# Attention kernel on eight cores: at each head change the next head's key and value expansion is placed behind the current step's work on the tensor engine

## The chip, the cores and the metric

The kernel runs on all 8 cores of one Trainium2 chip. There is no communication between the cores: each works on its own 1024 query rows. The metric is device time in microseconds (us) of the slowest core, lower is better. A core has five engines with a queue each, which run side by side and meet through semaphores: TensorE (PE, with its weight loads listed apart as PEld), VectorE (DVE), ScalarE (ACT), GpSimd (POOL) and SyncE (SP).

## The reference

One layer on x of shape (2, 4096, 4096): latent attention with 32 heads, then a gated low-rank feed-forward, each followed by a residual add and a layer norm. The part around the change:

```python
q = _rmsnorm(x @ wq_a.T) @ wq_b.T                 # 32 heads of 128
ckv, k_pe = split(x @ wkv_a.T)                    # latent of 256, rope part of 64
kv = _rmsnorm(ckv) @ wkv_b.T                      # per head: 64 of k_nope, 128 of v
q_pe, k_pe = rope(q_pe), rope(k_pe)
k_full = concat([k_nope, broadcast(k_pe)])        # 128 per head
scores = einsum('bqhd,bkhd->bhqk', q_full, k_full) * softmax_scale
attn = softmax(where(causal, scores, min))
out = einsum('bhqk,bkhd->bqhd', attn, v)
x = layernorm(x + out @ wo.T)
x = layernorm(x + ffn(x))                         # router, top 16 of 64 experts, rank 8
```

## The kernel before

The kernel runs in stages divided by barriers of all engines: the latent of keys and values (A), the queries (B and C), attention (D), the output projection with the first layer norm, and the feed-forward. The change is in stage D alone. `K` and `V` are not stored for all heads; only the normalised latent `cnorm` (256 x 4096) is, and each head's keys and values are expanded from it shortly before they are used. `emit_expansion(h, bank)` does that in 8 blocks of 512 keys. A block has 2 matmuls for the 64 k_nope rows into the left half of a PSUM score bank, a copy of them on DVE into `Kf`, 8 matmuls for four 128-key pieces of V into the right half of the bank, and a copy of them on ACT into `Vx`. In each block PE waits for the copies of the block ahead, since both use the same bank. `Kf` and `Vx` have two buffers, by the parity of the head.

Attention itself is one flat list of steps, `iters`: 32 heads, 8 slots of 128 queries, and 1, 2, 3, 4, 1, 2, 3, 4 key blocks of 1024 for them, so 20 steps a head and 640 in all. Step r has four parts: QK(r), 2 matmuls of 512 columns into `scores[r % 2]` (`sA` or `sB`); exp(r), one ACT instruction of 128x1024 into `P_sb`; T(r), 8 transposes on PE into `ptP`; evac(r), a copy of them (with a mask in a slot's last step) into `PT_sb`, on DVE if r is even or the step is the last of its slot, otherwise on ACT; and PV(r), 8 matmuls of 128x129 that add up in `mix`. Behind a slot's last PV there is a finish: reciprocal and scaling on DVE, a transpose on PE, and a copy back into `Q` on DVE.

The order within each queue is the order in which the Python loop emits. Round r of the loop emits exp(r) on ACT, then QK(r+1), PV(r-1) and T(r) on PE, then the finish of r-1 if there is one, then evac(r). So QK runs one step ahead of the exp, and PV one step behind the transposes. Where steps r and r+1 belong to different heads (r = 19, 39, ...; 31 times), `emit_expansion` of the next head goes between exp(r) and QK(r+1). Its score bank is the one that QK(r+1) will write, so PE waits for exp(r-1) ahead of it. In this text the steps around such a head change are called by the numbers of the first one: step 18 is r-1 (neither first nor last in its slot, its evac is on DVE), step 19 is the head's last (evac with mask, on DVE), and steps 20 and 21 are the next head's first two.

Every instruction is recorded by one helper, so the profile gives line 267 for all; the tiles tell them apart. `sA`, `sB` in the output of a matmul is QK or the expansion, `mix` is PV (or, with `idn`, the finish), `ptP` is a transpose; `AR` is the SBUF arena that holds all the rest.

Of the kernel before, what the change touches and what calls it, by code (L numbers as in the profile page):

```python
# [294 lines left out]
def build(debug=False, race_detect=True, upto="F"):  # L295
# [56 lines left out]
    with ExitStack() as ctx:  # L352
        em = Em(nc, ctx)
        _LAST_EM[0] = em
        _emit(nc, em, d, ctx, debug, upto)
        _replay(nc, em, ctx)
# [3 lines left out]
def _emit(nc, em, d, ctx, debug, upto="F"):  # L360
# [332 lines left out]
    with ExitStack() as pctx:  # L693
# [9 lines left out]
        scores = [sA, sB]  # L703
# [27 lines left out]
        tok_exp = [None] * N  # L731
# [8 lines left out]
        def emit_expansion(h, bank):  # L740
            hp = h % 2
            war = tok_flash_done.get(h - 2)
            ev = []
            kn_ev = [None] * 8
            v_ev = [None] * 8
            em.waits("pe", [t_wkvb])
            for b in range(8):
                if b >= 1:
                    em.wait("pe", kn_ev[b - 1])
                for c in range(2):  # L750
                    em.opw("pe", [t_wkvb], "matmul", bank[0:64, 0:512],
                           wkvb_sb[c][:, h * 192: h * 192 + 64],
                           cnorm[c][:, b * 512:(b + 1) * 512],
                           start=(c == 0), stop=(c == 1))
                t_kn = em.mark("pe")
                em.waits("dve", [t_kn, war, t_init, t_init_p])
                em.op("dve", "tensor_copy", Kf[hp][0:64, b * 512:(b + 1) * 512],
                      bank[0:64, 0:512])
                kn_ev[b] = em.mark("dve")
                ev.append(kn_ev[b])  # L760
                if b >= 1:
                    em.wait("pe", v_ev[b - 1])
                for sub in range(4):
                    kk = b * 4 + sub
                    for c in range(2):
                        em.opw("pe", [t_wkvb], "matmul",
                               bank[:, 512 + sub * 128: 512 + sub * 128 + 128],
                               cnorm[c][:, kk * 128:(kk + 1) * 128],
                               wkvb_sb[c][:, h * 192 + 64: h * 192 + 192],
                               start=(c == 0), stop=(c == 1))  # L770
                t_v = em.mark("pe")
                em.waits("act", [t_v, war, t_init, t_init_p])
                dst = Vx[hp][:, b * 4 * VSTRIDE:(b + 1) * 4 * VSTRIDE]
                dst = dst.rearrange("p (s w) -> p s w", w=VSTRIDE)[:, :, 0:128]
                em.op("act", "copy", dst,
                      bank[:, 512:1024].rearrange("p (s w) -> p s w", w=128))
                v_ev[b] = em.mark("act")
                ev.append(v_ev[b])
            tok_exp_ready[h] = ev

        def emit_qk(it):
            cu = iters[it]
            par = it % 2
            hp = cu["h"] % 2
            if it - 2 >= 0:
                em.wait("pe", tok_exp[it - 2])
            em.waits("pe", tok_exp_ready.get(cu["h"], []))
            kb = cu["kb"]
            lhsQ = Q[:, cu["h"] * 1024 + cu["s"] * 128: cu["h"] * 1024 + cu["s"] * 128 + 128]
            for hh in range(2):  # L790
                em.op("pe", "matmul", scores[par][:, hh * 512:(hh + 1) * 512],
                      lhsQ, Kf[hp][:, kb * 1024 + hh * 512: kb * 1024 + hh * 512 + 512],
                      start=True, stop=True)
            tok_qk[it] = em.mark("pe")
# [4 lines left out]
        for r in range(N + 1):  # L799
            prev = iters[r - 1] if r >= 1 else None  # L800
            cur = iters[r] if r < N else None
            nxt = iters[r + 1] if r + 1 < N else None

            if cur is not None:
                par = r % 2
                em.wait("act", tok_qk[r])
                if r - 2 >= 0:
                    em.wait("act", tok_pvt[r - 2])
                em.op("act", "activation", P_sb[par][:], scores[par][:], AF.Exp,
                      scale=SCALE)  # L810
                tok_exp[r] = em.mark("act")

            if nxt is not None:
                if cur is not None and nxt["h"] != cur["h"]:
                    if r - 1 >= 0:
                        em.wait("pe", tok_exp[r - 1])
                    emit_expansion(nxt["h"], scores[(r + 1) % 2])
                emit_qk(r + 1)

            if prev is not None:  # L820
                parp = (r - 1) % 2
                sp = prev["s"] % 2
                em.wait("pe", tok_evac[r - 1])
                if prev["first"] and fin_done[sp] is not None:
                    em.wait("pe", fin_done[sp])
                em.waits("pe", [fin_act_prev[0]])
                hpp = prev["h"] % 2
                kbp = prev["kb"]
                for t in range(8):
                    em.opw("pe", [tok_evac[r - 1]], "matmul", pv_[sp],  # L830
                           PT_sb[parp][:, t * 128:(t + 1) * 128],
                           Vx[hpp][:, (kbp * 8 + t) * VSTRIDE:
                                     (kbp * 8 + t) * VSTRIDE + 129],
                           start=(prev["first"] and t == 0),
                           stop=(prev["last"] and t == 7))

            if cur is not None:
                em.wait("pe", tok_exp[r])
                if r - 2 >= 0:
                    em.wait("pe", tok_evac[r - 2])  # L840
                for t in range(8):
                    em.opw("pe", [tok_exp[r]], "transpose",
                           ptP[par][:, t * 128:(t + 1) * 128],
                           P_sb[par][:, t * 128:(t + 1) * 128], idn16[:])
            tok_pvt[r] = em.mark("pe")

            if prev is not None and prev["last"]:
                sp = prev["s"] % 2
                h_, sf = prev["h"], prev["s"]
                em.wait("dve", tok_pvt[r])  # L850
                if fin_pe_prev[0] is not None:
                    em.wait("dve", fin_pe_prev[0])
                em.op("dve", "reciprocal", rcp_c, pv_[sp][:, 128:129])
                em.self_edge("dve")
                em.op("dve", "tensor_tensor", att_tm, pv_[sp][:, 0:128],
                      rcp_c.broadcast_to((128, 128)), op=ALU.mult)
                t_fin = em.mark("dve")
                fin_done[sp] = t_fin
                em.waits("pe", [t_fin, fin_act_prev[0]])
                em.opw("pe", [t_fin], "transpose", atp, att_tm, idn16[:])  # L860
                t_atp = em.mark("pe")
                fin_pe_prev[0] = t_atp
                em.wait("dve", t_atp)
                em.op("dve", "tensor_copy",
                      Q[:, h_ * 1024 + sf * 128: h_ * 1024 + sf * 128 + 128],
                      atp)
                fin_act_prev[0] = em.mark("dve")
                if sf == NSLOT - 1:
                    tok_flash_done[h_] = fin_act_prev[0]

            if cur is not None:
                e = "dve" if (cur["last"] or r % 2 == 0) else "act"
                em.wait(e, tok_pvt[r])
                if cur["last"]:
                    fam = 0 if cur["s"] < 4 else 1
                    em.op(e, "tensor_tensor", PT_sb[par][:], ptP[par][:],
                          mask2[:, fam * 1024:(fam + 1) * 1024], op=ALU.mult)
                elif e == "act":
                    em.op(e, "copy", PT_sb[par][:], ptP[par][:])
                else:  # L880
                    em.op(e, "tensor_copy", PT_sb[par][:], ptP[par][:])
                tok_evac[r] = em.mark(e)

        em.barrier()
        if debug:
# [408 lines left out]
```

How the kernel before makes its waits and increments, by code:

```python
        def body(h):  # L264
            for entry in em.stream[e]:
                meth, args, kw, sem, n = entry[:5]
                ins = getattr(h, meth)(*args, **kw)
                for s, v in (entry[5] if len(entry) > 5 else ()):
                    ins._wait_ge(s, v)
                if sem is not None:
                    ins.then_inc(sem, n)
```

## Time and profile before

| | us |
|---|---|
| median of 2 timed runs | 4754.3 (4746.57 to 4762.03) |
| profiled execution, device time | 4605.99 |
| its span, slowest core (core 2) | 4604.3 |
| spans of the 8 cores | 4536.6 to 4604.3 |
| stage D on core 2, from the first expansion to the last finish | 1155 to 3400 |

The profile comes from one execution. Busy times are sums over instructions of an engine, and they overlap between engines. In the timeline a row is a group of like instructions in order of start: start in us from the start of the span, time it took, engine, operation, output and input, and count; in square brackets is the engine's idle time ahead of it, and what ended that.
### The profile page before, as it was taken

The page shows a single profiled execution, that of the slowest core. Times are in us where ns is not written, and L with a number is a line of the kernel's source. Part 1 is how long each engine was busy: PE and PEld are TensorE (multiplying, and loading weights), DVE is VectorE, ACT ScalarE, POOL GpSimd, SP SyncE. Part 2 cuts the span into 40 slices and gives each one's busy share as a digit, 9 for nine tenths or more (in the row PEclk, how much of TensorE's full clock was granted, in tenths as well). Part 3 has the DMA queues.
Part 4 walks back from the last instruction along what each step waited for, and adds up shares of the span by engine and source line. Part 5 has one row for each costly group of instructions (what it writes and reads, how often), then busy time and mean ns, then how long its engine had stood idle before and what let it go on. Part 6 is the DMA issues. An engine that isn't in the chain of part 4 may idle for free.

```text
span 4604.3 us, 53278 instructions; the slowest of 8 cores (4536.6 to 4604.3 us)
## 1 busy us (share of the span) xinstructions
PE 2833.6 (62%) x19214; PEld 1381.0 (30%) x19214; DVE 1019.7 (22%) x1923; ACT 1229.8 (27%) x1280; POOL 355.1 (8%) x466
## 2 busy tenths in 40 slices
PE   2772644444666676666666666666668888727650
PEld 0220211111333343333333333333333333302110
DVE  0110010000232323222322322223310000161117
ACT  0000001111444444444454444444420000000110
POOL 4431002233000000000000000000010000000000
PEclk9886877777899989999999999899999999957775
DMA  8877240001100000000000000000043333210003
GB/s 119 114 100 107 40 67 6 0 0 25 22 1 1 1 1 1 1 1 1 1 1 1 1 1 1 1 1 1 1 75 82 83 83 82 55 38 0 0 0 146
DMA packets 76490, 145.64 MB, mean 32 GB/s; under 512 B 12306, under 2 KB 53396, under 8 KB 70228
## 3 DMA queue, kind: packets, MB, share of 16 engines
q0 software_dynamic: 67792, 116.29, 15.6%
q1 hardware_dynamic: 8452, 25.95, 1.5%
q8 instruction: 169, 2.77, 0.2%
q14 instruction: 77, 0.63, 0.0%
HBM read 233.31 MB, written 16.78 MB: 54 GB/s over the span
## 4 chain that ended last, share of the span: by engine, by line
PEldq 32%; issue 18%; PEld 15%; DVE 15%; ACT 7%; DMA 4%; another core or an unknown queue 3%; DVEq 2%; POOL 2%; POOLq 2%; ACTq 1%; SPq 0%
PEldq L267 32%; DVE AR L267 15%; ACT AR L267 7%; PEld mix L267 4%; PEld psE L267 3%; PEld sA L267 3%; DVEq L267 2%; POOL AR L267 2%; POOLq L267 2%; PEld psL L267 1%; ACTq L267 1%; DMA AR<-wqbT 1%; DMA AR<-xoT 1%; DMA out<-AR 1%
## 5 line engine op out<-in xcount | busy, mean ns | idle before, releaser
L267 PE MATMUL sA<-AR 128*128 128x128 bf16 (+2 forms) x3200 | 527.4, 288 | 194.1 <-issue 58.0
L267 PE MATMUL mix<-AR 128*128 128x129 bf16 x5120 | 410.1, 223 | 260.8 <-DVEq L267 172.9
L267 PE MATMUL psE<-AR 128*128 128x512 bf16 x2048 | 479.1, 398 | 16.8 <-issue 10.5
L267 PEld LDWEIGHTS mix<-AR 128*128 128x128 bf16 x5120 | 312.1, 99 | 572.1 <-DVEq L267 375.2
L267 PE MATMUL ptP<-idn,AR 128*128 128x128 bf16 x5120 | 401.8, 223 | 37.6 <-ACTq L267 37.3
L267 ACT ACTIVATE AR<-sB,consts 128x1024 bf16<-128x1024 f32 x320 | 356.3, 1113 | 147.4 <-PEq L267 118.9
L267 ACT ACTIVATE AR<-sA,consts 128x1024 bf16<-128x1024 f32 x320 | 356.2, 1113 | 91.2 <-PEq L267 71.0
L267 ACT COPY AR<-ptP 128x1024 bf16<-128x1024 bf16 x192 | 194.3, 1012 | 638.6 <-PEq L267 638.6
L267 ACT ACTIVATE AR<-AR 128x1024 bf16<-128x1024 bf16 (+3 forms) x76 | 76.4, 1006 | 1043.5 <-DVEq L267 1043.5
L267 PEld LDWEIGHTS ptP<-idn,AR 128*128 128x128 bf16 x5120 | 322.6, 99 | 48.3 <-ACTq L267 48.1
L267 PEld LDWEIGHTS sA<-AR 128*128 128x128 bf16 (+1 forms) x3200 | 199.2, 101 | 413.0 <-issue 389.1
L267 PEld LDWEIGHTS psE<-AR 128*128 128x128 bf16 x2048 | 206.0, 102 | 290.1 <-issue 74.1
L267 DVE TENSOR_TENSOR AR<-ptP,AR 128x1024 bf16<-128x1024 bf16 x256 | 177.1, 692 | 375.6 <-PEq L267 367.5
L267 PE MATMUL psL<-AR 128*128 128x512 bf16 (+1 forms) x768 | 186.9, 409 | 90.3 <-DMA AR<-xT 83.5
L267 ACT CAST AR<-sA 128x512 bf16<-128x512 f32 x256 | 149.8, 585 | 334.7 <-PEq L267 334.7
L267 DVE CAST AR<-sA 64x512 bf16<-64x512 f32 x256 | 174.8, 683 | 266.2 <-PEq L267 260.4
L267 DVE COPY AR<-ptP 128x1024 bf16<-128x1024 bf16 x192 | 132.8, 692 | 418.6 <-PEq L267 410.8
L267 PE MATMUL sB<-AR 128*128 128x512 bf16 x640 | 201.2, 397 | 26.0 <-issue 0.2
L267 PE MATMUL psC<-AR 128*128 128x512 bf16 x512 | 174.2, 516 | 66.9 <-DMA AR<-wqbT 60.0
L267 PE MATMUL mix<-idn,AR 128*128 128x128 bf16 x256 | 55.8, 218 | 246.7 <-DVEq L267 246.7
L267 POOL DMA_DIRECT2D AR<-A_sta x32 | 16.9, 664 | 2244.5 <-DVEq L267 2244.5
L267 PE MATMUL psB<-AR 128*128 128x512 bf16 x512 | 114.3, 385 | 107.0 <-DMA AR<-wqaT 107.0
(91 smaller groups left out, 1733.1 us busy)
## 6 DMA issues: line engine op xcount, KB each, us to landing
AR<-xT POOLq DMA_DIRECT2D x256, 128.0 KB, 11.4
AR<-wo_sta POOLq DMA_DIRECT2D x32, 1024.0 KB, 8.6
AR<-xoT SPq DMA_DIRECT2D x32, 512.0 KB, 8.3
AR<-xoT POOLq DMA_DIRECT2D x32, 256.0 KB, 21.7
AR<-wqaT POOLq DMA_DIRECT2D x4, 2048.0 KB, 69.1
AR<-wqbT POOLq DMA_DIRECT2D x8, 1024.0 KB, 29.8
out<-AR SPq DMA_DIRECT2D x16, 512.0 KB, 2.6
out<-AR POOLq DMA_DIRECT2D x16, 512.0 KB, 2.9
```

Of the source, the lines that this page charges most:

```text
L267: ins = getattr(h, meth)(*args, **kw)
```

## The change

At a head change the expansion of the next head and QK(r+1) move from ahead of PV(r-1) and T(r) to the end of the round, behind PV(r-1), T(r) and the emission of evac(r). Nothing is added or removed, and all other rounds are as they were. On PE the order at a head change goes from expansion, QK(20), PV(18), T(19), QK(21) to PV(18), T(19), expansion, QK(20), QK(21). On DVE evac(19) goes from behind the 8 key copies to ahead of them. The order on ACT stays.

```diff
-            if nxt is not None:
-                if cur is not None and nxt["h"] != cur["h"]:
-                    if r - 1 >= 0:
-                        em.wait("pe", tok_exp[r - 1])
-                    emit_expansion(nxt["h"], scores[(r + 1) % 2])
+            boundary = (nxt is not None and cur is not None
+                        and nxt["h"] != cur["h"])
+            if nxt is not None and not boundary:
                 emit_qk(r + 1)
 
             if prev is not None:
@@
                     em.op(e, "tensor_copy", PT_sb[par][:], ptP[par][:])
                 tok_evac[r] = em.mark(e)
+
+            if boundary:
+                if r - 1 >= 0:
+                    em.wait("pe", tok_exp[r - 1])
+                emit_expansion(nxt["h"], scores[(r + 1) % 2])
+                emit_qk(r + 1)
```

## Rows read from the trace of the kernel before

**Rows 1.** The page: its first line, and the busy times of all engines.

```profile
span 4604.3 us, 53278 instructions; the slowest of 8 cores (4536.6 to 4604.3 us)
PE 2833.6 (62%) x19214; PEld 1381.0 (30%) x19214; DVE 1019.7 (22%) x1923; ACT 1229.8 (27%) x1280; POOL 355.1 (8%) x466
```

**Rows 2.** Busy time by stretch, core 2: from second to last expansion, with column heads.

```profile
core 2: us, PE busy (x) PEld busy (x) DVE busy (x) ACT busy (x) POOL busy (x), PEclk, DMA share, GB/s
1230.27:3325.89 2095.62, 1400.84 (x13440) 814.26 (x13441) 618.85 (x1380) 990.52 (x1021) 0.00 (x0) 0.97 0.00 1
```

**Rows 3.** Waits of PE in the same stretch: total us, times, longest us.

```profile
PE mix L267 <- DVEq L267: 392.2, 618, 1.3
PE ptP L267 <- ACTq L267: 34.7, 58, 0.9
```

**Rows 4.** Timeline of core 2 into one head change, PE, ACT and DVE.

```profile
1998.93 0.60 PE L267 MATMUL sB<-AR 128*128 128x512 bf16 x2
1998.96 1.01 ACT L267 COPY AR<-ptP 128x1024 bf16<-128x1024 bf16 x1 [3.83 <-PEq L267]
2000.07 1.11 ACT L267 ACTIVATE AR<-sA,consts 128x1024 bf16<-128x1024 f32 x1
...
2000.13 0.62 PE L267 MATMUL mix<-AR 128*128 128x129 bf16 x8 [0.61 <-ACTq L267]
...
2001.34 1.11 ACT L267 ACTIVATE AR<-sB,consts 128x1024 bf16<-128x1024 f32 x1 [0.16 <-issue]
2001.35 0.61 PE L267 MATMUL ptP<-idn,AR 128*128 128x128 bf16 x8 [0.59 <-ACTq L267]
...
2002.04 1.31 PE L267 MATMUL sA<-AR 128*64 128x512 bf16 x10
2002.08 0.69 DVE L267 COPY AR<-ptP 128x1024 bf16<-128x1024 bf16 x1 [4.48 <-PEq L267]
...
2002.96 0.68 DVE L267 CAST AR<-sA 64x512 bf16<-64x512 f32 x1 [0.19 <-issue]
2003.52 0.59 ACT L267 CAST AR<-sA 128x512 bf16<-128x512 f32 x1 [1.07 <-PEq L267]
```

**Rows 5.** Timeline of core 2 behind that expansion.

```profile
2016.23 0.59 PE L267 MATMUL sA<-AR 128*128 128x512 bf16 x2 [0.87 <-ACTq L267]
...
2016.90 0.63 PE L267 MATMUL mix<-AR 128*128 128x129 bf16 x8
2016.94 1.11 ACT L267 ACTIVATE AR<-sA,consts 128x1024 bf16<-128x1024 f32 x1 [0.88 <-PEq L267]
...
2017.37 0.61 PE L267 MATMUL ptP<-idn,AR 128*128 128x128 bf16 x8
...
2018.06 0.60 PE L267 MATMUL sB<-AR 128*128 128x512 bf16 x2
2018.11 0.69 DVE L267 TENSOR_TENSOR AR<-ptP,AR 128x1024 bf16<-128x1024 bf16 x1 [2.77 <-PEq L267]
...
2018.98 0.62 PE L267 MATMUL mix<-AR 128*128 128x129 bf16 x8 [0.31 <-DVEq L267]
...
2019.44 0.61 PE L267 MATMUL ptP<-idn,AR 128*128 128x128 bf16 x8
```

**Rows 6.** Busy time by stretch, core 2: three heads, from expansion to next expansion.

```profile
1230.27:1298.71 68.44, 45.10 (x449) 26.34 (x449) 20.62 (x46) 33.01 (x35) 0.00 (x0) 1.00 0.00 1
...
1645.21:1725.30 80.09, 57.69 (x448) 32.46 (x449) 20.63 (x46) 32.61 (x35) 0.00 (x0) 0.77 0.00 1
...
2975.37:3052.63 77.26, 54.65 (x449) 30.66 (x449) 20.63 (x46) 32.62 (x35) 0.00 (x0) 0.82 0.00 1
```

**Rows 7.** Busy time by stretch, core 2: ahead of an expansion, behind it, and around another one.

```profile
2000.75:2004.15 3.40, 2.17 (x21) 1.19 (x20) 1.37 (x2) 2.13 (x3) 0.00 (x0) 1.00 0.00 0
2020.05:2023.45 3.40, 1.72 (x19) 1.13 (x19) 1.38 (x4) 0.00 (x0) 0.00 (x0) 1.00 0.00 0
...
1643.10:1683.80 40.70, 31.62 (x188) 16.95 (x186) 10.06 (x20) 12.92 (x16) 0.00 (x0) 0.56 0.00 0
```

## The prediction

> **What bounds the kernel now.** I read the page first, for the share of each engine. TensorE is the busiest, 2833.6 of 4604.3 us, 62% [rows 1], and no other engine passes 27%. So neither a pure engine limit nor a queue full of work sets the time; it is the order in which engines wait for one another. The change touches attention alone, so I then took the windows view over 30 whole heads, from the second expansion (1230.27) to the last (3325.89): 2095.62 us, of which PE is busy 1400.84, 67% [rows 2]. A head there costs 69.9 us on average. PE is the engine that everyone meets at, and the waits view says what it stands for: 392.2 us ahead of PV or a finish, until DVE is done, and 34.7 us ahead of transposes, until ACT is done [rows 3]. Each time PE is the next to run, so an added wait of PE is added time, and a removed one is time gained, unless another wait takes its place.
>
> Last I took the timeline around one head change. The reader is to name the steps in it. QK(19) starts at 1998.93, PV(17) at 2000.13, exp(18) runs from 2000.07 to 2001.18, T(18) from 2001.35 to 2001.96, exp(19) from 2001.34 to 2002.45, and the expansion begins at 2002.04 with no wait at all [rows 4]. Its last V copy releases QK(20) at 2016.23. Then come PV(18) at 2016.90, T(19) at 2017.37, QK(21) at 2018.06, PV(19) at 2018.98 behind a wait of 0.31 us for evac(19), and T(20) at 2019.44 [rows 5]. The two places between which I count are the start of the expansion slot, 2002.04, and the start of T(20), 2019.44. Before 2002.04 both kernels run the same order. From T(20) on they do so again, and the other engines have nothing older left to do by then: exp(20) is over, and evac(19) too. Today the distance is 2019.44 - 2002.04 = 17.40 us. The same pattern is met at all 31 head changes, since 20 steps a head make the parity of step 19 the same each time.
>
> **The change part by part.** Nothing is computed more or less. What moves is PV(18), T(19) and evac(19), forward over an expansion.
>
> First, what now stands ahead of the expansion. PV(18) needs evac(18). T(18) ends at 2001.96 and evac(18) runs on DVE from 2002.08 to 2002.77 [rows 4]. From the end of such a copy to the PV that waited for it the trace has 0.18 us: evac(19) ends at 2018.11 + 0.69 = 2018.80, PV(19) starts at 2018.98 [rows 5]. So PV(18) can start at 2002.95, which is 0.91 us later than the place in which the expansion starts today. Today this copy is free, because the expansion covers it; the cover is gone, and nothing else is put into the gap. QK(20), which covers it in an ordinary round, isn't there, as the keys of the next head don't exist yet.
>
> Then T(19) follows 0.47 us behind PV(18), as today (2016.90 to 2017.37), and what comes behind T(19) starts 0.69 us after it (2017.37 to 2018.06) [rows 5]. T(19) needs exp(19), over at 2002.45 [rows 4], so it doesn't wait. The expansion starts at 2002.95 + 0.47 + 0.69 = 2004.11. That is 2.07 us late: 0.91 idle and 1.16 of moved work.
>
> Second, the expansion itself. I cost it as unchanged, 2016.23 - 2002.04 = 14.19 us [rows 4, 5]. The one thing that could touch it is DVE: in the new order evac(19) stands in front of the first key copy. But today evac(18) stands there, of the same 0.69 us, and starts at the same 0.04 us behind the start of the expansion (2002.08), with the first key copy behind it at 2002.96 [rows 4]. One copy takes the other's place. ACT has the same queue as before, and is free earlier in relation to the first V copy: exp(19) ends 1.7 us ahead of it instead of 1.07. V copies don't run earlier for that, since each ends an idle time that PE set. QK(20) so starts at 2004.11 + 14.19 = 2018.30.
>
> Third, what stands behind it. PE now has QK(20), QK(21), PV(19), T(20). QK(21) needs exp(19) and PV(19) needs evac(19), both long over, so the wait for evac(19) is gone: PV(19) starts 0.92 us behind QK(21) today, and 0.67 would do (below), so it costs 0.25. By PE alone T(20) comes after 0.67 (QK to what follows, 2016.23 to 2016.90), 0.67 again, and 0.47, so 1.81 us after QK(20). But T(20) needs exp(20), which starts 0.71 us after QK(20) does (2016.94 less 2016.23), takes 1.11 [rows 5], and releases a transpose 0.17 us after its end (2001.18 to 2001.35) [rows 4]: 1.99 us. ACT decides, by 0.18 us. Today PV(18), T(19), QK(21) and PV(19) stand in between, 3.21 us in all, and exp(20) is well hidden. So T(20) starts at 2018.30 + 1.99 = 2020.29. The next ACT work, exp(21), starts 0.16 us after exp(20) ends, and T(21) needs it only more than 3 us after T(20) starts, because the finish of step 19 lies in between. Hidden.
>
> The sum for one head change: 0.91 idle ahead of PV(18), plus 0.18 for exp(20), less 0.25 for evac(19), plus 0.01 of rounding; or 2020.29 - 2019.44 = **+0.85 us**. The same instructions are run, so only these waits count. Times 31 it is +26 us. The end of attention is a barrier, and a later stage can't start earlier, so all of it reaches the end.
>
> For the bounds: if the exp is hidden after all and the waits cost nothing in passing, the sum is 0.91 - 0.25 = +0.66, 20 us. If the wait behind the evac costs as much as the largest of the PE waits for DVE, 1.3 us [rows 3], instead of 0.91, it is +1.24, 38 us.
>
> **Against its own time:** 4606.0 + 26 = 4632 us for a profiled execution like this one, span 4630. The timed runs of before are at 4754.3, 3.2% above the profiled one, and the trace doesn't show why. All terms are waits at fixed durations, so I add the same 26 us: 4780.3, a ratio of 1.0055.
>
> **The clock, weighed.** The heads' lengths differ by the granted clock. An undisturbed head takes 68.44 us at 1.00; two on core 2 took 80.09 at 0.77 and 77.26 at 0.82 [rows 6]. In the first of them the clock was at 0.56 over the 40.7 us that begin 2.1 us ahead of the expansion [rows 7], so at 1.2 GHz for most of the expansion and the steps behind it. Over the 30 heads the clock took 2095.62 - 30 x 68.44 = 42 us on this core. So it matters what the engine does ahead of an expansion. The 3.4 us behind PV(17), from 2000.75, hold 2.17 us of busy PE now, since the expansion begins in them [rows 7]; they will hold T(18), the gap of 0.91, PV(18) and T(19). With 0.61 for T(18) and 2003.42 + 0.61 - 2002.95 = 1.08 for the other two, that is 1.7 us. A stretch of the same length behind each expansion, 2020.05 to 2023.45, has 1.72 us and kept the clock at 1.00 here [rows 7]. So I expect no more falls than now. "TensorE: Matmul & The Clock Gate" of the Trainium skill, Part 4, says that a transpose "doesn't count as PE-busy the same way". By that rule the new stretch would be nearly empty but for PV(18), and the clock would fall there often; the trace doesn't decide it, since no stretch of it has so many transposes and so little else. By the row the sum stays +26 us, by the rule it would be that of the first rival.
>
> **The rivals.**
>
> *The clock falls at the head changes* (slower). Mechanism: the new gap of 0.91 us, with the two of 0.61 and 0.59 that are there already [rows 4], thins PE's work ahead of the expansion; the clock goes to 1.2 GHz, and the expansion and the first steps run at it. A price for one: 80.09 - 68.44 = 11.65 and 77.26 - 68.44 = 8.82, so about 10.2 us [rows 6]. At all 31 it is 317 us, 5097 in all. It decides from 7 heads on: 2% is 95 us, less my 26 leaves 69. For it: the fall shown began just ahead of an expansion. Against: the comparison in rows 7.
>
> *No net loss, or a small gain* (not slower). The wait for evac(18) comes out at no more than that for evac(19), since PV's weight loads run ahead and exp(20) is hidden: then -0.25 a head change, -8 us, 4746. Against it stands that T(18), evac(18), PV(18) form a chain of results in which nothing can run ahead. More than that isn't to be had: all idle of PE from the last V copy on is 0.87 + 0.31 = 1.18 us [rows 5], 37 us over 31, so under 0.8%. To be 2% faster a head change would have to give 3.07 us.
>
> *The clock falls less often* (a gain beside the sum). A head of another length meets the clock's falls at other places. If all 42 us went, the result would be 4780 - 42 = 4738.
>
> **How the numbers follow.** My forecast, a loss of 20 to 38 us with the clock about as now, gets 0.74. The gain or no loss gets 0.09, fewer falls of the clock 0.08, and more falls 0.09, of which 0.05 for seven or more. The predicted time is 4780.3. The range goes down to 4736, which takes in fewer falls and the small gain. Up it goes to 4825: 38 us instead of 26, and three heads with a long fall (31 us). Its own range, without the clock, is 4774 to 4792. Two per cent, 95 us, is about what a measurement of this kernel can tell from no change: faster by over 2% 0.02 (no mechanism reaches it), within 2% 0.93, slower 0.05.
>
> **What the profile of after would show.** Right: ahead of each expansion the order `sB`, `mix`, `ptP`, `mix`, `ptP`, then 80 matmuls on `sA`, with 0.9 to 1.0 us of PE idle ahead of the second `mix`, put down to DVE; behind the expansion QK on `sA` and `sB` back to back; PV(19) with no wait; T(20) with a wait of about 0.2 us for ACT; an undisturbed head at 69.3 us in place of 68.44; a span of stage D longer by about 26 us. Wrong in the first step: PV(18) starts less than 0.3 us behind T(18)'s end. Wrong in the second: expansions longer or shorter than 14.19 us at full clock. Wrong in the third: T(20) more than 2.3 or less than 1.8 us behind QK(20). Wrong on the clock: stretches at 0.5 that begin ahead of expansions in more than five heads of a core.

## The result

The changed kernel takes 4686.1 us (median of 11 runs, 4667.1 to 4828.1), the kernel before 4648.4 (median of 10 runs, 4593.4 to 4762.0). In four of the eleven runs the cores of one die had a lower granted clock than the others and took over 1% longer; every ratio in this text leaves such runs out, those of before too. The ratio is **1.0133**, with a 95% interval of 1.0069 to 1.0196. In a repeat on chip 15 (e8 below) it was 1.0158 (1.0131 to 1.0185). I had forecast 1.0055 and 4780.3 us, with a range from 4736. So the kernel did get slower, as forecast, but by 1.33%, about 62 us, where 26 were worked out. The absolute time lies below the range all the same, because the base that I added the 26 us to was too high.

The profiled execution took 4677.1 us, against 4606.0. The first line of the page of the kernel after, and its busy times, answer to [rows 1]. The spans and mean granted clock of its cores are from the cores view:

```profile
span 4675.5 us, 52991 instructions; the slowest of 8 cores (4647.9 to 4675.5 us)
PE 2827.9 (60%) x18896; PEld 1414.5 (30%) x19214; DVE 1019.6 (22%) x1923; ACT 1230.7 (26%) x1280; POOL 355.9 (8%) x466
```

```profile
core 0: 4675.5 us, clock 0.859
...
die 0 (median of its cores): 4668.2 us, clock 0.859
die 1 (median of its cores): 4656.2 us, clock 0.863
```

No engine has more to do than before. All eight cores are longer, and their clock is at 0.86. On core 2 before, the mean was 0.873, and 0.88 on most of the others.

Next is the timeline of core 0 after, around one head change at full clock. It answers to [rows 4, 5].

```profile
2673.28 1.11 ACT L267 ACTIVATE AR<-sB,consts 128x1024 bf16<-128x1024 f32 x1 [0.16 <-issue]
2673.29 0.61 PE L267 MATMUL ptP<-idn,AR 128*128 128x128 bf16 x8 [0.59 <-ACTq L267]
2674.02 0.69 DVE L267 COPY AR<-ptP 128x1024 bf16<-128x1024 bf16 x1 [4.48 <-PEq L267]
...
2674.89 0.62 PE L267 MATMUL mix<-AR 128*128 128x129 bf16 x8 [0.99 <-DVEq L267]
...
2675.35 0.61 PE L267 MATMUL ptP<-idn,AR 128*128 128x128 bf16 x8
...
2676.04 1.31 PE L267 MATMUL sA<-AR 128*64 128x512 bf16 x10
2676.09 0.69 DVE L267 TENSOR_TENSOR AR<-ptP,AR 128x1024 bf16<-128x1024 bf16 x1 [1.37 <-PEq L267]
...
2676.96 0.68 DVE L267 CAST AR<-sA 64x512 bf16<-64x512 f32 x1 [0.19 <-issue]
...
2690.80 0.60 PE L267 MATMUL sB<-AR 128*128 128x512 bf16 x2
2690.84 1.11 ACT L267 ACTIVATE AR<-sA,consts 128x1024 bf16<-128x1024 f32 x1 [0.88 <-PEq L267]
...
2691.48 0.63 PE L267 MATMUL mix<-AR 128*128 128x129 bf16 x8
...
2692.12 0.61 PE L267 MATMUL ptP<-idn,AR 128*128 128x128 bf16 x8
```

The reader finds the new order and each step of the sum. T(18) starts at 2673.29, PE stands 0.99 us for evac(18), and PV(18), T(19) and the expansion (2676.04) follow. evac(19) runs in the place that evac(18) had, and the first key copy starts 0.92 us behind the start of the expansion, as before. QK(21) at 2690.80 and PV(19) follow with no wait, and T(20) at 2692.12 starts 0.17 us after exp(20) has ended.

The windows view of core 0 after shows what the sum lacked. The rows are the 30 heads from the second to the last expansion (compare [rows 2]), one head (compare [rows 6]), and two stretches: one around the start of the next expansion at 2748.83, and one that begins 20 us behind the head's own.

```profile
1235.61:3393.62 2158.01, 1404.14 (x13230) 846.29 (x13441) 618.75 (x1380) 991.36 (x1020) 0.00 (x0) 0.94 0.00 1
2676.04:2748.83 72.79, 47.44 (x442) 28.75 (x449) 20.62 (x46) 33.04 (x34) 0.00 (x0) 0.92 0.00 1
2747.10:2750.50 3.40, 3.24 (x24) 2.10 (x23) 1.19 (x2) 0.00 (x0) 0.00 (x0) 0.50 0.00 0
...
2695.90:2702.70 6.80, 4.73 (x32) 2.69 (x30) 1.38 (x4) 3.24 (x3) 0.00 (x0) 0.50 0.00 0
```

This head took 72.79 us where I expected 69.3. TensorE ran at 1.2 GHz 20 us behind its expansion, where slots end in short steps and PE waits for one finish after another, and again from 1.7 us ahead of the next expansion, in the new gap. The 30 heads took 2158.01 us at a clock of 0.94, against 2095.62 at 0.97 [rows 2] on a core that was the worst of its eight.

To compare whole kernels I counted falls. A fall is a stretch at 1.2 GHz in the trace's record of the granted clock, from the second to the last expansion. The figures are means over the eight cores of the one profiled execution of each kernel. An "undisturbed head" is the median of those heads with no fall in them.

| kernel | undisturbed head, us | mean head, us | falls a core | us at 1.2 GHz a core |
|---|---|---|---|---|
| before | 68.38 | 68.97 | 10.4 | 61 |
| after | 68.83 (5 heads of 240) | 71.73 | 57.4 | 253 |

Mean by mean, the 30 heads went from 2069 to 2152 us. That is 83 us, and the mean span went from 4576.2 to 4661.6, which is 85. So the loss is in attention, and not in the stages around it.

### The profile page after: what moved, and what is told of

Read it like the earlier page. It is cut to its first block, busy times and chain, and to the rows that moved or that the text cites. A ratio compares the mean times of both kernels' runs of the same rounds, so it can differ in the third digit from the quotient of the medians.

```text
span 4675.5 us, 52991 instructions; the slowest of 8 cores (4647.9 to 4675.5 us)
## 1 busy us (share of the span) xinstructions
PE 2827.9 (60%) x18896; PEld 1414.5 (30%) x19214; DVE 1019.6 (22%) x1923; ACT 1230.7 (26%) x1280; POOL 355.9 (8%) x466
## 4 chain that ended last, share of the span: by engine, by line
PEldq 32%; issue 17%; PEld 15%; DVE 14%; ACT 8%; DMA 5%; POOL 2%; DVEq 2%; POOLq 2%; ACTq 1%; another core or an unknown queue 1%; SPq 0%
PEldq L267 32%; DVE AR L267 14%; ACT AR L267 8%; PEld mix L267 4%; PEld psE L267 3%; PEld sA L267 3%; POOL AR L267 2%; DVEq L267 2%; POOLq L267 2%; PEld psL L267 1%; ACTq L267 1%; PEld ptP L267 1%; DMA AR<-xT 1%; DMA AR<-wqbT 1%
## 5 line engine op out<-in xcount | busy, mean ns | idle before, releaser
L267 PE MATMUL sA<-AR 128*128 128x128 bf16 (+2 forms) x3072 | 507.2, 287 | 220.1 <-issue 86.4
L267 PE MATMUL mix<-AR 128*128 128x129 bf16 x5120 | 424.8, 228 | 276.4 <-DVEq L267 190.6
L267 PEld LDWEIGHTS mix<-AR 128*128 128x128 bf16 x5120 | 322.8, 101 | 587.9 <-DVEq L267 387.3
L267 PE MATMUL ptP<-idn,AR 128*128 128x128 bf16 x5120 | 422.3, 229 | 36.0 <-ACTq L267 35.5
L267 PEld LDWEIGHTS ptP<-idn,AR 128*128 128x128 bf16 x5120 | 340.3, 103 | 51.3 <-ACTq L267 51.1
L267 PE MATMUL sB<-AR 128*128 128x512 bf16 x544 | 185.6, 410 | 48.9 <-issue 30.8
L267 ACT CAST AR<-psC 64x1024 bf16<-64x1024 f32 x64 | 64.4, 1007 | 431.1 <-PEq L267 430.7
```

The costliest lines, as they stand in the source:

```text
L267: ins = getattr(h, meth)(*args, **kw)
```

## The experiments

The kernel before ran beside them on the same chip each time (4595.2 us in the first series, 4596.7 in the second, 4601.8 in the third). "Dummies" are matmuls with 512 columns of the identity with `cnorm`, written to the score bank that the next real matmul overwrites. The result of the kernel is unchanged by them, and they cost 0.21 us each where nothing hides them (16 of them lengthen the undisturbed head by 3.30 us in e11 below).

### Is it the gap, or the length of the head?

The kernel after has two new traits: a gap of 0.9 us ahead of PV(18), and a head that is about 0.8 us longer. Either could bring the falls.

**e1_dense_pad**: the length without the gap, in the order of before.

```diff
                         em.wait("pe", tok_exp[r - 1])
+                    dummies(scores[(r + 1) % 2], 4)
                     emit_expansion(nxt["h"], scores[(r + 1) % 2])
```

> The kernel before, with 4 matmuls of 512 columns added ahead of each head change's expansion; their result is overwritten. It lengthens an undisturbed head from 68.4 us to about 69.3, as the change does, but with dense work, no gap and the old order. Two theories on why TensorE's granted clock falls about 59 times a core in the kernel after and about 10 times before. The gap theory (the 0.9 us of idle ahead of PV(18)): about 10 falls a core as before, mean head 69.3 to 70.2, total +27 to +35 us against before (ratio 1.006 to 1.008). The head-length theory (a head of 69.3 us meets the clock's falls at other places than one of 68.4): 40 to 60 falls a core, mean head 71 to 72, total +60 to +90 us.

Measured: ratio 1.0147 (1.0128 to 1.0167), 4661.4 us against 4595.2. Undisturbed head 69.00 us, mean head 70.78, 26.9 falls a core, 168 us at 1.2 GHz. Only 3 of 215 falls lie over 66 us behind an expansion, where the gap would be; 154 lie 19 to 24 us behind one. Four dense matmuls that add 0.6 us to an undisturbed head cost 1.8 us a head. The gap isn't needed for a good part of the loss. But 27 falls are half of after's 57, and fewer than the 40 to 60 of the length theory, so the length isn't all of it either.

**e2_gap_filled**: the length and the order of after, with the gap filled.

```diff
             if prev is not None:
+                if boundary:
+                    dummies(scores[(r + 1) % 2], 4)
                 em.wait("pe", tok_evac[r - 1])
```

> The kernel after, with the same 4 matmuls placed between T(18) and PV(18) in each head change, where TensorE waits 0.9 us for evac(18). The head's length should stay at about 69.3 us; only the gap is filled. Gap theory: falls of the clock back to 10 to 15 a core, mean head 69.3 to 70, total 30 to 50 us under after. Head-length theory: 40 to 60 falls a core as in after, total as after within 15 us, with only the falls just ahead of the expansions gone.

Measured: ratio 1.0156 (1.0126 to 1.0187), 4661.0 us. Undisturbed head 69.08, mean head 70.97, 31.2 falls a core, 185 us at 1.2 GHz; 3 of 250 falls are ahead of an expansion, against 162 of 459 in after. So the gap makes those, and they go with it. The rest stays as in the dense pad. Neither theory had it right alone. Timed, the gain is less clear: the ratio lies within the interval of after's, and the median is 17 us under the 4677.9 of after, measured on another chip.

**e3_gap_only**: the gap in the order of before. PE waits for evac(18) and goes straight into the expansion.

```diff
                         em.wait("pe", tok_exp[r - 1])
+                        em.wait("pe", tok_evac[r - 1])
                     emit_expansion(nxt["h"], scores[(r + 1) % 2])
```

> The kernel before with its order kept, and one wait more: TensorE waits for evac(18) ahead of the expansion. So the gap of 0.9 us stands where the change puts it, and PV(18) and T(19) stay behind the expansion. Undisturbed head about 69.3 us. Both theories give many falls here, 40 to 60 a core, and +60 to +90 us against before. If there are about 10 instead, neither the gap nor the length makes them, and the new order of PV(18), T(19), QK(21) does; then +28 us.

Measured: ratio 1.0519 (1.0466 to 1.0572), 4824.1 us. 58.8 falls a core, as both theories had it, but 583 us at 1.2 GHz, and a mean head of 75.18 us where the undisturbed one is 69.01. I hadn't foreseen the size: +229 us from one wait of 1 us, where 60 to 90 were expected. What differs from after is where the falls begin. The windows and the timeline of core 0:

```profile
2976.50:3000.40 23.90, 19.27 (x101) 9.38 (x100) 6.06 (x9) 6.09 (x10) 0.00 (x0) 0.50 0.00 1
...
2975.70:3054.24 78.54, 55.61 (x449) 31.32 (x450) 20.63 (x46) 33.02 (x34) 0.00 (x0) 0.80 0.00 1
```

```profile
2974.10 0.61 PE L267 MATMUL ptP<-idn,AR 128*128 128x128 bf16 x8 [0.59 <-ACTq L267]
2975.70 1.65 PE L267 MATMUL sA<-AR 128*64 128x512 bf16 x10 [0.99 <-DVEq L267]
2977.58 1.03 PE L267 MATMUL sA<-AR 128*64 128x512 bf16 x2 [0.23 <-issue]
```

The fall begins 0.8 us behind the start of the expansion, and the clock stays at 0.50 for 23.9 us, to its end and past it. 167 of this kernel's 470 falls begin within 5 us behind an expansion's start, and 121 of the 470 last 23.9 us; in before and after no fall begins within those 5 us. In after, PV(18) and T(19) stand between gap and expansion, and most falls there are over when the expansion has hardly begun (0.50 from 2747.10 to 2750.50, above).

**e4_long_head**: the kernel after, gap kept, with 11 dummies (2.4 us) ahead of each expansion.

```diff
             if boundary:
+                dummies(scores[(r + 1) % 2], 11)
                 emit_expansion(nxt["h"], scores[(r + 1) % 2])
```

> The kernel after, gap kept, with 11 matmuls of 512 columns ahead of each expansion (2.4 us of dense work): undisturbed head about 71.7 us. Head-length theory: the number of falls depends on the length, so it will differ much from 59 a core, and about 10 to 20 are expected at this length; then the mean head is about 72.3 and the total only 10 to 30 us over after, although 31 x 2.4 = 74 us of work were added. Gap theory: falls as in after, 50 to 60 a core, and the total 70 to 80 us over after.

Measured: ratio 1.0331 (1.0312 to 1.0349), 4750.1 us, 72 us over the 4677.9 of after further down (on another chip). Undisturbed head 71.30, mean head 73.90, 48.8 falls a core. The forecast of the length theory, 10 to 20 falls and 10 to 30 us over after, failed here. As the gap is still there (145 of 390 falls over 66 us behind an expansion), this kernel can't tell whether length matters by itself; that needed a series without a gap.

### The length alone, in a series

The dense pad again with 2, 8 and 16 dummies in place of 4.

> The kernel before with 2 dense matmuls of 512 columns ahead of each expansion instead of the 4 of the dense pad (which had 27 falls of the clock a core against 10 before). Undisturbed head about 68.7 us. If the length of a head decides how often its thin places meet a fall, 10 to 25 falls a core, between the two. If it was only the presence of the added work, about 27.

> The same with 8 matmuls, undisturbed head about 70 us. Length theory: at least as many falls as with 4, 25 to 50 a core. Otherwise 27 or fewer, as nothing is thinner than with 4.

> The same with 16 matmuls, undisturbed head about 71.6 us. Length theory: the number of falls doesn't simply grow with the length; the four cases 68.4, 68.7, 70 and 71.6 us differ, and this one is at 5 to 15 falls a core again. If falls rise steadily with the length or stay at 27, the length alone isn't the reason, or not by meeting a beat.

| kernel | dummies | undisturbed head, us | mean head, us | falls a core | us at 1.2 GHz |
|---|---|---|---|---|---|
| before | 0 | 68.38 | 68.97 | 10.4 | 61 |
| e9_pad_2 | 2 | 68.55 | 69.86 | 22.0 | 122 |
| e1_dense_pad | 4 | 69.00 | 70.78 | 26.9 | 168 |
| e10_pad_8 | 8 | none | 71.84 | 38.6 | 204 |
| e11_pad_16 | 16 | 71.68 | 72.01 | 9.2 | 41 |

The profiled executions took 4621.0, 4680.7 and 4692.4 us with 2, 8 and 16 dummies, so all three are slower than the 4601.8 of before; the falls came as the length theory had them. With 8 dummies no head of 240 is without a fall; with 16, 191 are. The last 8 dummies, 1.7 us of work a head, cost 0.17 us of mean head. The windows view of core 2 of that kernel, with the clock back at 0.99 over its 30 heads:

```profile
1241.69:3404.80 2163.11, 1428.26 (x13682) 844.52 (x13921) 618.36 (x1380) 991.36 (x1020) 0.00 (x0) 0.99 0.00 1
```

So dense work that opens no gap changes how often the clock falls, and not by "more is worse". What all these kernels have in common is the thin places in a head, where slots end in short steps (19 to 24 and 47 to 53 us behind an expansion, 73 of 83 falls in before). How often the clock falls there changes with what the dummies do to the head, and the length is what I changed on purpose: 68.4 us has few falls, 71.7 has few again, and between them is no length with few that I tried. The length is still argued and not shown. For it is e2, where the dummies stand elsewhere and the head has e1's length: 31 falls against 27. Against it is e4: at 71.30 us it has 245 falls outside the gap, 31 a core, where e11 has 9 at 71.68, so 0.4 us would have to make that difference, or the falls in the gap bring others with them. Why one length should meet more falls than another stays open.

### What is left with the clock out of the way

**e5_fill_finish**: the kernel before, with the thin places filled. Nothing else is changed.

```diff
                 fin_done[sp] = t_fin
+                if cur is not None:
+                    dummies(scores[par], 3)
                 em.waits("pe", [t_fin, fin_act_prev[0]])
```

> The kernel before, order kept, with 3 matmuls of 512 columns (result overwritten) in each of the 256 places where TensorE waits 0.95 us for DVE's finish of a slot. They lie inside a wait, so an undisturbed head should stay at 68.4 us. Clock theory (falls begin where TensorE is thinly used): the falls around 20 and 50 us behind an expansion, 73 of 83 before, vanish; 0 to 3 a core are left, mean head 68.4 to 68.6, total 10 to 25 us under before. If the falls have another cause, they stay at 10 a core and the total is the same or a little longer.

Measured: ratio **0.9909** (0.9886 to 0.9932), 4556.3 us against 4596.7. No fall in any head of any core; mean head 68.29 us. This is the fastest kernel of the case, ahead of both before and after. The cores agree within 27 us now, and the heads' window of core 4 reads:

```profile
1221.07:3270.96 2049.89, 1502.86 (x13950) 840.91 (x14161) 618.40 (x1380) 990.54 (x1021) 0.00 (x0) 1.00 0.00 1
```

It gains 40 us by doing more: PE is busy 1502.86 us in 30 heads, and 1400.84 in [rows 2]. I had expected 10 to 25 us. On the mean of the cores the 30 heads shrank by 20 us (2069 to 2049), but on the slowest core by 46 (2095.62 to 2049.89), and the slowest core is what is timed. Some 9 us between these profiles lie ahead of attention (first expansion at 1142.7 on average against 1152.0) and aren't owed to the dummies.

**e6_after_all_filled**: the kernel after with the fillings of both e2 and e5.

> The kernel after, with 4 such matmuls in the 0.9 us gap ahead of PV(18) and 3 in each finish wait. If the change costs its waits (+0.85 us a head change) and the clock the rest, this has 0 to 5 falls a core, a mean head of 69.2 to 69.4, and a total 15 to 30 us over before (ratio 1.003 to 1.007), and 25 to 35 us over the kernel before with filled finishes. If the waits are worth more than I worked out, the ratio stays at 1.012 or above although the clock no longer falls.

Measured: ratio 1.0005 (0.9987 to 1.0023), 4596.0 us. No fall in the heads, mean head 69.07. The time is that of before, not 15 to 30 us over it, as the fillings gain more than I had expected. The window of core 2:

```profile
1249.52:3321.50 2071.98, 1535.14 (x14070) 850.48 (x14281) 618.62 (x1380) 991.37 (x1020) 0.00 (x0) 1.00 0.01 1
```

e6 against e5 isolates the waits. The two differ by the change and by dummies that lie in its gap: 69.07 - 68.29 = 0.78 us a head, 24 us in 31. The medians differ by 40 us; in the profiles 15 of them lie ahead of attention, where the first expansion starts at 1142.7 us on average in one profile and at 1158.1 in the other (it is at 1152 to 1154 in before and after), so they don't belong to the change.

**e8_after_again**: the kernel after beside them.

> The kernel after once more, unchanged, beside the others on the same chip. Both theories: ratio 1.013 to 1.022 to before, 50 to 60 falls a core, 3 of 10 of them just ahead of an expansion. The difference to the kernel with gap and finishes filled is what the clock costs: 45 to 65 us are expected.

Measured: ratio 1.0158 (1.0131 to 1.0185), 4677.9 us, mean head 71.55, 56.2 falls a core. It is 82 us over e6, where I had expected 45 to 65; 74 of them are in the 30 heads (2146 less 2072, means over the cores).

**e12_gap_left**: e6 with the gap open again.

> The kernel after with the finish waits filled, as in the kernel without a single fall, but the 0.9 us gap ahead of PV(18) left open. If the gap by itself lets the clock fall, 10 to 25 falls a core, nearly all 66 to 72 us behind an expansion, so just ahead of the next, mean head 69.4 to 70. If the gap only does so in heads that are disturbed already, 0 to 3 falls and a mean head of 69.1.

Measured in one execution: 4592.6 us, 10.4 falls a core, 45 us at 1.2 GHz, mean head 69.56 us. All 83 falls lie over 66 us behind an expansion. Windows of core 6, its 30 heads and one of the falls, with the next expansion at 3164.32:

```profile
1219.56:3302.95 2083.39, 1567.99 (x14160) 849.56 (x14161) 618.79 (x1380) 991.60 (x1020) 0.00 (x0) 0.99 0.00 1
3163.00:3166.40 3.40, 3.24 (x23) 1.93 (x20) 1.38 (x2) 0.00 (x0) 0.00 (x0) 0.50 0.02 5
```

So the gap lets the clock fall by itself, in one head of three, for 0.5 us a head (69.56 - 69.07). The time of the whole kernel doesn't show these 15 us against the 4596.0 of e6, since the first expansion starts at 1141.5 us here and at 1158.1 there. In after the clock falls there in two heads of three (162 falls over 66 us behind an expansion, in 240 heads). That falls elsewhere in the head bring the others about is a guess; no run shows it.

### Could the moved work be hidden?

**e7_woven**: PV(18) and T(19) inside the expansion.

```diff
+                emit_expansion(nxt["h"], scores[(r + 1) % 2],
+                               {(0, "v"): pv_part,
+                                (1, "kn"): lambda: t_part(0, 4),
+                                (1, "v"): lambda: t_part(4, 8)})
+                emit_qk(r + 1)
```

> The kernel before with PV(18) and T(19) neither ahead of nor behind the expansion but inside it, in waits that TensorE has there anyway: PV(18) behind the V part of block 0, T(19) in halves around the V part of block 1. By the waits alone: the expansion stays near 14.2 us, T(20) follows QK(20) by 2.0 us, so an undisturbed head falls from 68.4 to about 67.2 us, 38 us in all, ratio 0.992. By the head-length theory a head of 67.2 us may meet more falls of the clock than one of 68.4, as the one of 69.3 did: then 25 or more falls a core and a ratio of 0.998 to 1.005 in spite of the shorter head.

Measured: ratio 1.0001 (0.9976 to 1.0027), 4599.1 us, undisturbed head 68.14, mean head 68.73, 12.5 falls a core. The head shrank by 0.24 us and not by 1.2. The timeline of core 5 shows why, with an expansion that starts at 1372.23:

```profile
1373.78 0.62 PE L267 MATMUL mix<-AR 128*128 128x129 bf16 x8 [0.23 <-issue]
...
1374.37 0.59 PE L267 MATMUL sA<-AR 128*64 128x512 bf16 x2
...
1375.27 0.38 PE L267 MATMUL ptP<-idn,AR 128*128 128x128 bf16 x4 [0.31 <-issue]
...
1376.81 0.59 PE L267 MATMUL sA<-AR 128*64 128x512 bf16 x2 [0.23 <-issue]
```

The same two blocks in before, core 2, whose expansion starts at 2002.04 [rows 4]:

```profile
2003.82 0.59 PE L267 MATMUL sA<-AR 128*64 128x512 bf16 x2 [0.47 <-DVEq L267]
...
2005.48 0.59 PE L267 MATMUL sA<-AR 128*64 128x512 bf16 x2 [0.23 <-DVEq L267]
```

Block 1 starts 2.14 us behind the expansion's start, against 1.78 before, and block 2 4.58 us, against 3.44. From the expansion's start to QK(20) it is 15.17 us (median of 237 head changes at full clock), against 14.17 before, so 1.0 of the 1.2 us was lost inside the expansion. The pieces that are woven in are marked for other engines one by one, and the rows have an idle 0.2 to 0.3 us ("issue") ahead of most of them; that these make up the whole 1.0 isn't shown. The falls stayed low at this length; the theory's warning of 25 or more didn't come true.

## Why the prediction was wrong, point by point

**The sum of the waits was right.** The prediction had +0.85 us a head change: 0.91 idle ahead of PV(18), 0.18 for exp(20), less 0.25 for evac(19). At full clock, the time from T(18) to T(20) is 18.84 us in after (median of 84 head changes) and 18.06 in before (246): +0.77. By parts: T(18) to the expansion 2.75 against 0.69, so +2.06 (forecast 2.07); the expansion with QK(20), up to what follows, 14.77 against 14.84 (forecast: unchanged); from there to T(20) 1.32 against 2.54, so -1.22 (forecast 1.99 against 3.21 from QK(20) on, also -1.22). With the clock taken out, e6 against e5, it is +0.78 a head, 24 us for 31. I had said 26.

**The step that failed is the clock, in "So I expect no more falls than now".** The falls went from 10.4 to 57.4 a core. Filled kernels give the size: the clock costs 2069 - 2049 = 20 us in the 30 heads of before, and 2152 - 2072 = 80 in those of after. So of the 83 us that the heads grew in the profiles, 23 are waits and 60 are clock. Timed, the difference is 62 us by the first ratio and 73 by the second; by each of the three the clock is the larger part. An estimate splits the 60: the gap's part is 71.73 - 70.97 = 0.76 us a head (after against e2), 23 us in 30 heads, and what the dense pad shows without a gap is (70.78 - 69.00) - (68.97 - 68.38) = 1.19 us a head, 36 us.

I compared one stretch of 3.4 us ahead of the expansion with one behind it and found them equally busy [rows 7]. The comparison was true. The new stretch holds 1.73 us of busy PE in after, where 1.7 was worked out and 1.72 compared with it:

```profile
2672.69:2676.09 3.40, 1.73 (x26) 1.44 (x26) 0.69 (x2) 1.55 (x2) 0.00 (x0) 1.00 0.00 0
```

The conclusion was wrong, for two reasons. The stretch behind the expansion was itself one of the places where the clock falls (34 of 83 falls in before begin 19 to 24 us behind an expansion); it was at 1.00 in the one head that I looked at. And I never asked what another head length does to the falls that are there: I named it only as a gain, "the clock falls less often". A count of the falls in before by place would have shown the first, and a series like the one above the second.

**The rival with the falling clock** had a right mechanism, the gap ahead of the expansion, for part of the loss, but a wrong price. I took 10.2 us from two long falls [rows 6]. Of after's 162 falls at the gap 156 are over within 13.7 us, 154 of them within 3.4, and only six last 37.5 to 41.0 us; e12 puts the gap at 0.5 us a head. The long sort is what e3 has, where the expansion itself stands behind the gap, and there the clock costs 75.18 - 69.01 = 6.2 us a head on average, nearer to the rival's price. Between PV(17) and the expansion, the gap's stretch has 16 transposes and 8 matmuls, and in e12 the clock stood in two such stretches of three. On the rule of the Trainium skill ("TensorE: Matmul & The Clock Gate", Part 4) that a transpose "doesn't count as PE-busy the same way", the clock would fall there often, as the prediction has it; one in three is fewer than a nearly empty stretch would suggest, and more than the 34 in 240 heads of the equally busy stretch in before, so the runs don't decide it.

**The small gain** didn't come, as forecast: nothing hid evac(18).

**The base.** 4780.3 was 4754.3 + 26. The two runs behind 4754.3 turned out to be the slowest of ten, whose median is 4648.4. I had seen that they were 3.2% above the profiled execution, gave no reason, and built on them all the same. That put the forecast 106 us too high, and this alone took the result out of the range. Against its own time the sum came to 4632 for a profiled execution, where 4677 was measured: 45 us too low, which is the clock. So the two errors point opposite ways. On the median of all ten the sum would have given 4674, 12 us from the 4686.1 measured, and that would have been luck, with the clock's part still missing.

## What to carry to other kernels

Before an edit that adds a small wait on TensorE or alters a loop's length, count the falls of its granted clock by place over the whole trace; one stretch at full clock proves nothing. Where falls sit in short waits for another engine, a few dummy matmuls inside those waits lengthened no undisturbed head and took all falls away here (e5), for 0.9%, more than the 0.8% that the prediction put as the most the edit could gain. And when work is moved past a stage that can't overlap, ask what that stage used to hide: here a copy of 0.69 us.

## What the runs showed of the hardware that I had not expected

Dense work that isn't needed made a kernel faster (e5, 4556 against 4597 us, with about 100 us more of busy PE in 30 heads). The number of falls neither rises nor sinks steadily with the dense work added to a head: 10, 22, 27, 39 and 9 a core for 0, 2, 4, 8 and 16 added matmuls. And a wait of 1 us cost 7.4 us a head change (229 us over 31) where an expansion with waits of its own follows it at once (e3, with falls of 23.9 us), but 0.5 us of clock a head where PV(18) and T(19) stand between it and the expansion and the other thin places are filled (e12).
